# Two moves in the attention loop: ScalarE's high parts ahead of its copy of the transposed outputs, VectorE's shifted row ahead of the sums of squares

## The chip, the cores and the metric

The kernel runs on one core of one Trainium2 chip. The metric is the device time of one execution in microseconds (us), from 3 executions of the kernel before: 829.25, 830.49 and 831.02, so a median of 830.49.

## The reference, cut to what matters

The input `x` is 128 sequences of 64 tokens with 256 channels, and `cond` has one row of 256 per sequence. The reference is `x` plus one transformer block in which each linear layer stands between a log map and an exp map of hyperbolic space:

```
xn = layer_norm(logmap0(x))
xm = expmap0(xn * (1 + sc_msa) + sh_msa)
q, k, v = (_to_heads(plin(xm, w, b)) for w, b in ((w_q, b_q), (w_k, b_k), (w_v, b_v)))
scores = einsum('bhqd,bhkd->bhqk', logmap0(q), logmap0(k)) / sqrt(HD)
out_h = expmap0(einsum('bhqk,bhkd->bhqd', softmax(scores), logmap0(v)))
attn_out = plin(_from_heads(out_h), w_o, b_o)
x = mobius_add(residual, expmap0(g_msa * logmap0(attn_out)))
...
```

There are 16 heads of 16 channels. After the first half comes a second one of the same kind with two feed-forward layers. Every `logmap0` and `expmap0` needs the norm of a row, or of each head's 16 channels in a row; this is why the kernel sums squares by head and takes inverse roots.

## The kernel before, in words

Two sequences make a tile of 128 rows, so there are 64 tiles, and all of `x` stays in SBUF. The program has a set-up (weights, the modulation rows of `cond`, statistics of `x`), a first half (attention, tile by tile), a short stage of arithmetic for all rows at once, and a second half (feed-forward, two tiles at a time). The change touches the first half alone.

The first half is a software pipeline written out by hand. A slot is one step of it, and in each slot every stage works on another tile: with lag 0 (`L_A`) the layer norm's `modulate` and `shift_t`, with lag 1 (`L_B`) the transposes of `t`, with lag 2 (`L_C`) the projection to q, k and v, with lag 3 (`L_D`) `project`, `square_u`, `sum_squares`, `sum_rows`, `inverse_norms` and `head_roots`, with lag 4 (`L_E`) `limit`, `factors`, `scale_qk`, `high_parts`, `low_parts` and `repeat_parts`, with lag 5 (`L_H`) the transposes of q and k, the scores, the exponential and `attend`, with lag 6 (`L_L`) `softmax_sums`, `normalise`, `evac_oT` and the output projection, with lag 7 (`L_G`) the gate and the statistics. Each engine runs its own list of these calls in a fixed order, and an instruction waits on semaphores for what other engines (or its own earlier instructions) have made. So the order of the calls in `slot` (ScalarE, GpSimd, TensorE) and in `slot_until_rows` and `slot_from_bias` (VectorE) sets the order of the work.

Slots 0 to 7 and the last ones are written out; those between are a loop of two slots per pass. VectorE's loop is rotated: it is turned between the two parts of an even slot, so that the jump back (the instructions of L311) stands right behind `sum_rows` of each even slot and ahead of `gate_z`; an odd slot has no jump inside.

What the two moves and their neighbours do:

- `high_parts` (L614, ScalarE) rounds the scaled q and k (`qk`) to 16-bit floats in `qk4`. `low_parts` (L477, GpSimd) subtracts these from `qk` and stores the rests. `repeat_parts` (L1236 and L1237, VectorE) copies both to their second places, and only then can TensorE transpose them (L855), with which a slot begins on TensorE.
- `evac_oT` (L624, ScalarE) copies the transposed attention outputs out of PSUM, for the output projection (L872).
- `sum_squares` (L1167, VectorE) sums the squares that ScalarE made (`square_u`, L635) over each head's 16 channels, and `sum_rows` (L1171) sums those over the heads. ScalarE takes an estimate of the inverse roots of them (L646, L649), and GpSimd's five steps (L452, L454, L456, L458, L461) refine it to `roots`, which VectorE's `limit` (L1210) needs in the next slot.
- `modulate` (L1094, VectorE) writes `lnx`, and `shift_t` (L1145) makes `t` of it. It waits for `modulate` through the semaphore `ln_half`.
- `gate_z` (L1196, VectorE) multiplies the attention's result with the gate rows, with both inputs in SBUF; `dot_x` (L1203), `add_bo` (L1189) and `repeat_parts` follow.

```
dve.wait_ge(ln_half, i + 1)
...
dve.wait_ge(heads_summed, i + 1)
dve.tensor_reduce(hs[:, 3 * H:NF], hs[:, 0:3 * H].rearrange("p (a h) -> p a h", h=H), AX.X, ALU.add).then_inc(rows_summed, 1)
```

Of the kernel before, what the change touches and what calls it, by code (L numbers as in the profile page):

```python
# [52 lines left out]
def build(nc, x, cond, w_q, b_q, w_k, b_k, w_v, b_v, w_o, b_o, w_f1, b_f1, w_f2, b_f2, w_ada, b_ada, out):  # L53
# [16 lines left out]
    with ExitStack() as ctx:  # L70
# [216 lines left out]
        L_A, L_B, L_C, L_D, L_E, L_H, L_L, L_G = 0, 1, 2, 3, 4, 5, 6, 7  # L287
# [44 lines left out]
        def on(h, off, lag, items=T):  # L332

            return not isinstance(h, int) or 0 <= 2 * h + off - lag < items
# [222 lines left out]
        def _(act):  # L557
# [74 lines left out]
            def square_u(i, k):  # L632
                act.wait_ge(u_ready, i + 1)
                after(act, heads_summed, i)
                act.activation(usq[:, :], u[:, k, :], ACT.Square).then_inc(u_squared, 1)  # L635
# [33 lines left out]
            def slot(h, off):  # L669
                if on(h, off, L_H):  # L670
                    evac_qkT(2 * h + off - L_H)
                if on(h, off, L_B):
                    evac_tT(2 * h + off - L_B, (off - L_B) % 2)
                if on(h, off, L_D):
                    square_u(2 * h + off - L_D, (off - L_D) % 2)
                if on(h, off, L_L):
                    evac_oT(2 * h + off - L_L)
                if on(h, off, L_E):
                    high_parts(2 * h + off - L_E)
                if on(h, off, L_H):  # L680
                    exp_scores(2 * h + off - L_H)
                if on(h, off, L_D):
                    inverse_norms(2 * h + off - L_D)
                if on(h, off, L_A):
                    square_t(2 * h + off - L_A, (off - L_A) % 2)
                if on(h, off, L_G):
                    square_zg(2 * h + off - L_G, (off - L_G) % 2)
                if on(h, off, L_L):
                    square_z(2 * h + off - L_L, (off - L_L) % 2)

            run_tiles(act, slot)

            def scale_x(i, j):
# [303 lines left out]
        def _(dve):  # L997
# [241 lines left out]
            def slot_until_rows(h, off):  # L1239
# [11 lines left out]
                    scale_qk(2 * h + off - L_E, (off - L_E) % 2)  # L1251
                if on(h, off, L_A) and not at_start(h, off):
                    modulate(2 * h + off - L_A, (off - L_A) % 2, h + (off - L_A) // 2)
                if on(h, off, L_D):
                    sum_squares(2 * h + off - L_D)
                if on(h, off, L_A):
                    shift_t(2 * h + off - L_A, (off - L_A) % 2)
                if on(h, off, L_D):
                    sum_rows(2 * h + off - L_D)

            def slot_from_bias(h, off):
# [272 lines left out]
```

## Time and profile before

| what | value |
|---|---|
| median of 3 executions | 830.49 us |
| the profiled execution's own time | 829.5 us |
| its span in the profile | 827.7 us |
| granted TensorE clock, mean | 0.956 of full speed |
| busy share VectorE, TensorE (matmul), ScalarE, GpSimd | 86%, 84%, 70%, 43% |
| first half in its loop | about 95 to 500 us |

The profile is of one execution. Its page gives the busy time of each engine and the costliest groups of instructions; the trace behind it also answers for a stretch of time: each instruction's start and duration, who waited for whom, and the chain of work that ended last. PE is TensorE's matmul, PEld its load of weights, DVE VectorE, ACT ScalarE, POOL GpSimd; "DVEq" is VectorE's sequencer, which runs jumps and register instructions. An instruction of an engine can start shortly before the one ahead of it has ended, since they are pipelined.

### The profile page before, as it was taken

What the parts mean: (1) busy time and instruction counts of PE and PEld (TensorE: products, weight loads), DVE (VectorE), ACT (ScalarE), POOL (GpSimd) and SP (SyncE); (2) the same over time, 40 slices, a digit from 0 to 9 for tenths busy, and PEclk for the clock granted to TensorE, in tenths of its full rate; (3) what the DMA queues carried; (4) which work ended last, traced back from release to release, by engine and by line L of the source; (5) the groups of instructions that cost most, each with busy time, mean ns of one, the idle gap of its engine ahead of it and who ended that gap; (6) DMA issues with size and microseconds to landing.
All of it is one profiled execution on the core that took longest, in us unless ns stands there. A gap on an engine that the chain in (4) does not pass through costs nothing.

```text
span 827.7 us, 29731 instructions
## 1 busy us (share of the span) xinstructions
PE 691.9 (84%) x9393; PEld 514.0 (62%) x9393; DVE 715.3 (86%) x2231; ACT 580.6 (70%) x1627; POOL 355.9 (43%) x682
## 2 busy tenths in 40 slices
PE   5957999898999989999899999623778999889996
PEld 2746777777777777777777777511335555555555
DVE  3767899999999999999999999866988888888885
ACT  1125787777877777777778777633668888878874
POOL 1005555565555655555655556310233233233231
PEclk9969999999999999999999999955989999999999
DMA  9931111111112111111111110022343555455533
GB/s 325 358 83 61 39 54 58 57 55 46 51 57 57 57 45 52 55 57 57 49 50 53 57 57 21 24 68 65 86 116 109 136 153 145 127 136 154 143 100 102
DMA packets 51811, 73.99 MB, mean 89 GB/s; under 512 B 7081, under 2 KB 34609, under 8 KB 51762
## 3 DMA queue, kind: packets, MB, share of 16 engines
q1 hardware_dynamic: 49970, 70.55, 29.1%
q10 hardware_dynamic: 1792, 2.89, 1.0%
q8 instruction: 18, 0.29, 0.2%
q14 instruction: 31, 0.25, 0.1%
HBM read 64.24 MB, written 9.18 MB: 89 GB/s over the span
## 4 chain that ended last, share of the span: by engine, by line
issue 30%; PE 19%; DVE 19%; ACT 12%; DVEq 4%; DMA 3%; POOL 2%; SPq 1%; ACTq 0%; POOLq 0%
PE p_s L855 8%; ACT usq L635 5%; PE p_s L963 3%; ACT tT L630 3%; DVEq L50 2%; DMA mod_b<-mod_rows 2%; DVE qk L1237 2%; PE p_qkv L963 2%; DVE g_all L1196 1%; PE p_t L949 1%; DVE t L1145 1%; PE p_o L977 1%; PE p_o L976 1%; PE p_o L975 1%; DVE junk L1203 1%
## 5 line engine op out<-in xcount | busy, mean ns | idle before, releaser
L898 PE MATMUL p_qkv<-wqkv,tT 128*128 128x256 f32 x768 | 189.9, 385 | 2.0 <-DVE u L1161 2.0
L898 PEld LDWEIGHTS p_qkv<-wqkv,tT 128*128 128x128 f32 x768 | 136.4, 193 | 19.1 <-ACT tT L630 2.4
L477 POOL TENSOR_TENSOR qk<-qk 128x512 f16<-128x512 f32 x64 | 74.1, 1158 | 100.4 <-ACT qk L614 100.4
L619 ACT ACTIVATE qkT<-p_s 128x1024 f32<-128x1024 f32 x64 | 65.5, 1024 | 73.7 <-PE p_s L855 73.7
L855 PE MATMUL p_s<-ident,qk 128*128 128x128 f16 x1024 | 69.1, 221 | 32.7 <-DVE qk L1237 32.7
L912 PEld LDWEIGHTS p_o<-v,pT 64*64 64x64 f32 x4096 | 68.2, 136 | 36.0 <-issue 36.0
L912 PE MATMUL p_o<-v,pT 64*64 64x17 f32 x4096 | 72.6, 209 | 12.2 <-ACT pT L666 12.2
L855 PEld LDWEIGHTS p_s<-ident,qk 128*128 128x128 f16 x1024 | 58.0, 98 | 38.8 <-DVE qk L1237 38.7
L666 ACT ACTIVATE pT<-p_s 128x1024 f32<-128x1024 f32 x64 | 65.5, 1024 | 19.8 <-PE p_s L888 19.7
L1196 DVE SCALAR_TENSOR_TENSOR g_all<-z,gate 128x256 f32 (+1 forms) x64 | 63.9, 998 | 13.1 <-issue 13.1
L872 PE MATMUL p_oz<-wo,oT 128*128 128x256 f32 x256 | 74.2, 413 | 0.9 <-ACT oT L624 0.9
L1227 DVE TENSOR_TENSOR qk<-u,fac 128x256 f32<-128x256 f32 x128 | 70.5, 589 | 0.1
L445 POOL TENSOR_TENSOR rt<-ss_t,c_mhalf 128x1 f32<-128x1 f32 x64 | 46.8, 730 | 53.8 <-ACT junk L641 53.8
L504 POOL TENSOR_TENSOR rt<-ss,c_mhalf 128x2 f32<-128x2 f32 x32 | 24.3, 761 | 101.2 <-ACT wqkv L716 99.4
L1161 DVE SCALAR_TENSOR_TENSOR u<-p_qkv,ct,bqkv 128x768 f32<-128x768 f32 x64 | 64.3, 1005 | 2.9 <-PE p_qkv L898 2.9
L1167 DVE TENSOR_REDUCE hs<-usq 128x48 f32<-128x768 f32 x64 | 61.0, 952 | 4.0 <-ACT usq L635 1.6
L963 PE MATMUL p_qkv<-wff,qk 128*128 128x384 f32 (+1 forms) x128 | 58.8, 608 | 3.7 <-ACT qk L728 3.6
L949 PE MATMUL p_t<-ident,pT 128*128 128x128 f32 x128 | 20.7, 286 | 47.7 <-ACT pT L723 47.7
L510 POOL TENSOR_TENSOR rh<-hh,c_mhalf 128x2 f32<-128x2 f32 x32 | 26.3, 820 | 74.2 <-DVE hh L1381 74.2
L468 POOL TENSOR_TENSOR v<-u,fac 128x256 f32<-128x256 f32 x64 | 40.3, 629 | 36.2 <-DVE fac L1216 36.2
L963 PE MATMUL p_s<-wff,qk 128*128 128x384 f32 (+1 forms) x128 | 52.4, 552 | 4.1 <-ACT qk L728 4.1
L635 ACT ACTIVATE usq<-u 128x768 f32<-128x768 f32 x64 | 54.1, 846 | 0.8 <-DVE u L1161 0.8
(268 smaller groups left out, 1720.4 us busy)
## 6 DMA issues: line engine op xcount, KB each, us to landing
mod<-mod_rows SPq DMA_DIRECT2D x128, 128.0 KB, 2.9
x_all<-in_x SPq DMA_DIRECT2D x8, 1024.0 KB, 14.2
gate<-mod_rows SPq DMA_DIRECT2D x128, 64.0 KB, 2.5
mod<-mod_rows SPq DMA_DIRECT2D x32, 256.0 KB, 4.1
mod_b<-mod_rows SPq DMA_DIRECT2D x32, 256.0 KB, 4.1
out<-x_all SPq DMA_DIRECT2D x32, 256.0 KB, 2.2
gate<-gate_rows SPq DMA_DIRECT2D x32, 128.0 KB, 3.4
bqkv<-gate_rows SPq DMA_DIRECT2D x32, 128.0 KB, 3.9
```

The source lines that it names most:

```text
L477: pool.tensor_tensor(low, qk[:, :].rearrange("p (a h d) -> p a h d", a=2, d=HD), qk4[:, :, :, 0, :], ALU.subtract).then_inc(low_ready, 1)
L619: act.activation(qkT[:, :, :, :].rearrange("p a g n -> p (a g n)").bitcast(F32), p_s[:, :], ACT.Copy).then_inc(qkT_ready, 1)
L635: act.activation(usq[:, :], u[:, k, :], ACT.Square).then_inc(u_squared, 1)
L666: act.activation(pT[:, :, :, :].rearrange("p e g n -> p (e g n)"), p_s[:, :], ACT.Exp, scale=SCALE / (QK_UP * QK_UP)).then_inc(p_ready, 1)
L855: mm = pe.transpose(p_qkT[:, a, g, :], qk4[:, a, 2 * g:2 * g + 2, :, :].rearrange("p h r d -> p (h r d)"), ident16[:, :])
L872: mm = pe.matmul(p_oz[:, 0:D], oT[:, c, :, :].rearrange("p b s -> p (b s)"), wo[:, c, :], start=c == 0, stop=c == C - 1)
L898: mm = pe.matmul(p_qkv[:, a * D:a * D + D], tT[:, k, c, :], wqkv[:, c, a * D:a * D + D], start=c == 0, stop=c == C - 1)
L912: mm = pe.matmul(p_o[S * e:S * e + S, col:col + VW], pT[keys, e, g, :], v[keys, k, 2 * g + e, :], start=True, stop=True, skip_group_check= ...
L963: mm = pe.matmul((p_qkv, p_s)[k][:, 512 * j + c * P:512 * j + 512], t2T[:, k, j, c, :], wff[:, c, c * P:2 * D], start=False, stop=c == C - 1)
L1161: dve.scalar_tensor_tensor(out=u[:, k, :], in0=p_qkv[:, 0:3 * D], scalar=ct[:, k:k + 1], in1=bqkv[:, :], op0=ALU.mult, op1=ALU.add).then_i ...
L1196: dve.scalar_tensor_tensor(out=tile_of(g_all, i), in0=z[:, :], scalar=1.0, in1=gate[:, k, :], op0=ALU.mult, op1=ALU.mult, accum_out=st[:, ...
L1227: dve.tensor_tensor(qk[:, part].rearrange("p (h d) -> p h d", d=HD), u[:, k, part].rearrange("p (h d) -> p h d", d=HD), fac[:, a * H:a * H ...
```

## The change

ScalarE now makes the high parts before it copies the transposed outputs. VectorE now makes `t` right behind `lnx`, and the sums of squares behind `t`. No instruction is added or taken away, none changes its size, and no wait is changed.

```diff
@@ ScalarE, slot
                 if on(h, off, L_D):
                     square_u(2 * h + off - L_D, (off - L_D) % 2)
+                if on(h, off, L_E):
+                    high_parts(2 * h + off - L_E)
                 if on(h, off, L_L):
                     evac_oT(2 * h + off - L_L)
-                if on(h, off, L_E):
-                    high_parts(2 * h + off - L_E)
                 if on(h, off, L_H):
                     exp_scores(2 * h + off - L_H)
@@ VectorE, slot_until_rows
                 if on(h, off, L_A) and not at_start(h, off):
                     modulate(2 * h + off - L_A, (off - L_A) % 2, h + (off - L_A) // 2)
-                if on(h, off, L_D):
-                    sum_squares(2 * h + off - L_D)
                 if on(h, off, L_A):
                     shift_t(2 * h + off - L_A, (off - L_A) % 2)
                 if on(h, off, L_D):
+                    sum_squares(2 * h + off - L_D)
                     sum_rows(2 * h + off - L_D)
```

VectorE's list before, in an odd slot of the loop, from `modulate` to `gate_z` (ISA and REGISTER_ALU are instructions of the sequencer):

```order
L1094 SCALAR_TENSOR_TENSOR lnx<-x_all,arrays,mod 128x256
L1167 TENSOR_REDUCE hs<-usq 128x48 [waits roots_ready,u_squared]
L1142 REGISTER_ALU
L1145 ISA [waits t_squared,tT_psum,ln_half]
L1145 SCALAR_TENSOR_TENSOR t<-lnx,arrays,mod 128x256
L1171 TENSOR_REDUCE hs<-hs 128x3 [waits heads_summed]
L1194 ISA [waits z_ready]
L1196 ISA [waits stats_kept,gate_in0]
L1196 SCALAR_TENSOR_TENSOR g_all,st<-z,gate 128x256
```

The same place in the changed kernel:

```order
L1094 SCALAR_TENSOR_TENSOR lnx<-x_all,arrays,mod 128x256
L1142 REGISTER_ALU
L1145 ISA [waits t_squared,tT_psum,ln_half]
L1145 SCALAR_TENSOR_TENSOR t<-lnx,arrays,mod 128x256
L1167 TENSOR_REDUCE hs<-usq 128x48 [waits roots_ready,u_squared]
L1171 TENSOR_REDUCE hs<-hs 128x3 [waits heads_summed]
L1194 ISA [waits z_ready]
L1196 ISA [waits stats_kept,gate_in0]
L1196 SCALAR_TENSOR_TENSOR g_all,st<-z,gate 128x256
```

The large sum (L1167) has moved behind `t` with nothing between it and the small sum that waits for it (L1171), and the sequencer's instruction that waits for `ln_half` now follows `lnx` directly.

ScalarE's list before, in the first slot of a pass of its loop:

```order
L635 ACTIVATE usq<-u 128x768 [waits heads_summed]
L50 REGISTER_ALU [waits oT_psum]
L624 ACTIVATE oT<-p_oz 128x2x2x64 [waits z_psum]
L610 ISA
L614 ACTIVATE qk<-qk 128x32x16 [waits low_ready,again_ready,qkT_psum,qk_ready]
L666 ACTIVATE pT<-p_s 128x1024 [waits o_psum,s_psum]
```

And in the changed kernel:

```order
L635 ACTIVATE usq<-u 128x768 [waits heads_summed]
L610 ISA
L614 ACTIVATE qk<-qk 128x32x16 [waits low_ready,again_ready,qkT_psum,qk_ready]
L50 REGISTER_ALU [waits oT_psum]
L624 ACTIVATE oT<-p_oz 128x2x2x64 [waits z_psum]
L666 ACTIVATE pT<-p_s 128x1024 [waits o_psum,s_psum]
```

The copy of the outputs, with the register instruction that waits for TensorE's transposes, has moved behind the high parts.

## Rows read from the trace of the kernel before

**Rows 1.** The page, busy time of each engine over the span.

```profile
PE 691.9 (84%) x9393; PEld 514.0 (62%) x9393; DVE 715.3 (86%) x2231; ACT 580.6 (70%) x1627; POOL 355.9 (43%) x682
```

**Rows 2.** Waits of 100 to 500 us: who for whom, total us, times, longest.

```profile
POOL qk L477 <- ACT qk L614: 88.3, 55, 1.7
```

**Rows 3.** Timeline of an odd slot: start us, us, engine, line, operation.

```profile
308.57 1.07 PE L855 MATMUL p_s<-ident,qk 128*128 128x128 f16 x16 [0.56 <-DVE qk L1237]
309.40 0.17 DVE L1210 TENSOR_TENSOR rlim<-roots,c_lim 128x3 f32<-128x3 f32 x1
310.86 0.85 ACT L635 ACTIVATE usq<-u 128x768 f32<-128x768 f32 x1
311.21 0.47 DVE L1094 SCALAR_TENSOR_TENSOR lnx<-x_all,arrays,mod 128x256 f32<-128x256 f32 x1
311.74 0.95 DVE L1167 TENSOR_REDUCE hs<-usq 128x48 f32<-128x768 f32 x1
311.85 0.38 ACT L624 ACTIVATE oT<-p_oz 128x256 f32<-128x256 f32 x1
312.13 0.62 ACT L614 ACTIVATE qk<-qk 128x512 f16<-128x512 f32 x1
...
312.98 1.16 POOL L477 TENSOR_TENSOR qk<-qk 128x512 f16<-128x512 f32 x1 [1.61 <-ACT qk L614]
313.12 1.30 DVE L1196 SCALAR_TENSOR_TENSOR g_all<-z,gate 128x256 f32 x1
314.35 0.08 DVE L1196 DVE_READ_ACCUMULATOR g_all<-z,gate 128x1 f32 x1
314.72 0.40 POOL L452 TENSOR_TENSOR nw<-y 128x51 f32<-128x51 f32 x1 [0.58 <-ACT y L649]
...
315.89 1.07 PE L855 MATMUL p_s<-ident,qk 128*128 128x128 f16 x16 [0.48 <-DVE qk L1237]
316.40 0.29 POOL L461 TENSOR_TENSOR roots<-nw,c_fac 128x51 f32<-128x51 f32 x1
316.72 0.17 DVE L1210 TENSOR_TENSOR rlim<-roots,c_lim 128x3 f32<-128x3 f32 x1
```

**Rows 4.** Timeline of the even slot before it, the same columns.

```profile
301.18 1.07 PE L855 MATMUL p_s<-ident,qk 128*128 128x128 f16 x16 [0.48 <-DVE qk L1237]
...
302.01 0.16 DVE L1210 TENSOR_TENSOR rlim<-roots,c_lim 128x3 f32<-128x3 f32 x1
303.92 0.47 DVE L1094 SCALAR_TENSOR_TENSOR lnx<-x_all,arrays,mod 128x256 f32<-128x256 f32 x1
304.42 0.95 DVE L1167 TENSOR_REDUCE hs<-usq 128x48 f32<-128x768 f32 x1
305.29 0.47 DVE L1145 SCALAR_TENSOR_TENSOR t<-lnx,arrays,mod 128x256 f32<-128x256 f32 x1
305.69 0.19 DVE L1171 TENSOR_REDUCE hs<-hs 128x3 f32<-128x48 f32 x1
306.36 0.74 DVE L1196 SCALAR_TENSOR_TENSOR g_all<-z,gate 128x256 f32 x1 [0.48 <-issue]
```

**Rows 5.** Line 311 from 304 to 308 us: operation, duration ns, start.

```profile
L311 DVEq ALU_OP  x1: 40/40/40, 305.4 to 305.4; - x1
```

**Rows 6.** Chain of waits, the sequencer's instruction ahead of the gate, even slot, then odd.

```profile
306.23 0.08 DVEq L1196
312.92 0.06 DVEq L1196
```

**Rows 7.** Lines 1196 and 456 over the span: duration ns min/median/max, first and last start.

```profile
L1196 DVE SCALAR_TENSOR_TENSOR g_all<-z,gate x64: 412/970/1423, 92.5 to 545.4; 128x256 f32 x54, 128x256 f32<-128x256 f32 x10
L456 POOL TENSOR_TENSOR nw<-nw,c_three x64: 275/407/412, 67.5 to 526.7; 128x51 f32<-128x51 f32 x64
```

## The prediction

> **What bounds the kernel now.** The page comes first [rows 1]: VectorE is busy for 86% of the span and TensorE for 84%, so neither can be called idle, and the shares don't say which wait ends last. The waits of the loop come next [rows 2]: GpSimd waits for the high parts 55 times, 88.3 us in all. That is a long wait of an engine that has time, and it says only that the low parts start as soon as they can. The timelines show what hangs on that start [rows 3, 4]. I read each as distances from T, the start of TensorE's transposes of q and k.
>
> In the odd slot T is 308.57 and the next T is 315.89, 7.32 us later. ScalarE's squares start at T+2.29, its copy of the outputs at T+3.28, the high parts at T+3.56. The low parts start 0.23 after these have ended, at T+4.41, and end at T+5.57. VectorE begins its gate product (L1196) at T+4.55, and it takes 1.30 us, where the shortest of its kind takes 0.41 [rows 7]. Its accumulator is read at T+5.78, 0.21 after the low parts have ended. So this product stands still while GpSimd runs, and from the read to the next T there are another 1.54 us of VectorE's work (the products and copies that end in L1237). The even slot has the same pattern and 7.39 us. **So the chain squares, copy, high parts, low parts, gate product sets the length of both slots**, and a pair of slots takes 14.71 us.
>
> A second chain is tied with it. GpSimd's five steps towards the roots start at T+6.15 and end at 316.69, and VectorE's `limit` follows at 316.72, which is T+8.15 and also 0.83 behind the next T [rows 3]. It has hardly any slack. Nothing that the change moves stands between T and those five steps (TensorE's order, the exponential), so this chain doesn't get shorter with the first.
>
> **ScalarE's move.** The high parts now start behind the squares. Neighbours on ScalarE overlap by 0.10 us (the copy, 0.38 long, starts 0.28 ahead of the high parts), so the high parts start at 2.29 + 0.85 - 0.10 = T+3.04, 0.52 earlier: 0.28 for the copy and 0.24 that the copy had waited for TensorE and for its issue. The low parts then run from 3.04 + 0.62 + 0.23 = T+3.89 to T+5.05. The copy of the outputs ends by T+3.94 instead of T+3.66. The projection that needs it starts at about T+4.4, behind the scores, and this covers the 0.28; without that cover it would be paid once in each slot.
>
> **VectorE's move, the odd slot.** `t` now follows `lnx` directly and needs its result. The sequencer's instruction that waits for it can run only when `lnx` has ended: I take 0.47 for `lnx`, 0.05 until the sequencer goes on (the large sum of the even slot ends at 305.37, and the sequencer's next instruction is at 305.4 [rows 4, 5]), 0.06 for its instruction and 0.05 until the engine starts (306.23 + 0.08 against 306.36 [rows 4, 6]). So `t` starts 0.63 behind `lnx`. The large sum follows 0.40 later (as L1171 behind L1145 [rows 4]) and takes 0.95. Before, the sum stood 0.53 behind `lnx`, so it now ends about 0.50 later. In the odd slot, with `lnx` at T+2.64, the sum ends at T+4.62. The gate product can start 0.34 after that (312.69 to 312.92 + 0.06 + 0.05 [rows 3, 6]), at T+4.96. The low parts end at T+5.05, so they still decide: accumulator at T+5.26, next T at 5.26 + 1.54 = **6.80, where it was 7.32**. `t` itself is read out before T+3.89, so it doesn't meet the low parts; the large sum does. The small sum ran 0.19 long beside the low parts [rows 4], so I don't charge the large one. The Trainium skill (SBUF — State Buffer, section "Who interferes with whom") says that a reduction never contends with GpSimd and that an instruction with two SBUF inputs does; the trace agrees for the small sum and the gate product, and if the large sum stood still as that product does, the odd slot would get no shorter at all.
>
> **The even slot.** Here the jump back of the loop lies between the small sum and the gate product. The jump's first instruction is at 305.4, right behind the end of the large sum (305.37), though `t` had been handed over long before: the sequencer stood at the small sum, which waits for the large one. From the end of the large sum to the gate product there are 0.99 us [rows 4]. Before, `t` ran inside this stretch and the low parts covered the rest. Now `t` is ahead of it and the stretch is bare. Counted from `limit`: `lnx` at +1.91, `t` 0.63, sum 0.40, its length 0.95, jump 0.99, so the gate product starts at +4.88 (before: 306.36 - 302.01 = +4.35). The low parts end near +4.1, so it runs unhindered: 0.34 to the accumulator, then 1.54, and the next T is at +6.76. Before it was 308.57 - 302.01 = +6.56. **The even slot becomes longer by 0.20, counted from `limit`.**
>
> **The sum.** With odd slots of 6.80 the even slot's `limit` no longer waits for VectorE (6.80 + 0.83 = T+7.63) but for the roots. Before they allowed T+8.15. Two of the five steps were slowed by VectorE's copies: the shortest L456 takes 0.28 and the median 0.41 [rows 7], and L452 took 0.40 [rows 3]. If nothing met any more, 0.25 would go: T+7.90. The copies now come 0.52 earlier beside the same steps and meet L452 and L454, so I expect one of the two delays to stay, T+8.00. A pair then takes 8.00 + 6.76 = 14.76 us against 14.71. The loop has 27 passes (slots 8 to 61), so + 0.05 x 27 = +1.4 us. The bounds are T+7.90 (pair 14.66, -1.4 us) and T+8.15 with one more 0.10 where a GpSimd step delays a copy (pair 15.01, +8 us).
>
> The slots that are written out have no jump. There the earlier low parts help, some 2 to 3 slots of them by 0.4: -1.0 us, with 0 and -2.1 (four slots by 0.52) as bounds. Against the profiled execution this gives 829.5 + 1.4 - 1.0 = 829.9; the median of the runs stands 1.0 higher, so 830.9, and I say 830.8.
>
> **Rivals.**
> - **A, the jump stays hidden: much faster.** If the sequencer hands over the small sum and runs the jump while that still waits, the even gate product waits for the low parts alone: the high parts at about +2.04 from `limit`, low parts to +4.05, accumulator +4.26, next T at +5.80. Two slots could then take 13.80. The chain through the roots, one `limit` to the next (309.40 to 316.72, 7.32), gives back perhaps 0.2 in a slot, so I take 14.2: -0.5 x 27 = -14 us, 816 us. Against it stands the jump at 305.4 [rows 5], which had no reason to wait until then except the sum. The Trainium skill (Perfetto Trace Analysis, section "DVE / Act Engine Instruction (TENSOR_ADD, Activation, etc)") says that an instruction is pushed into a wait queue and the sequencer is then ready to decode the next one; by that rule this rival would come true. The row speaks for a held sequencer.
> - **B, the roots are made earlier: a little faster.** If none of GpSimd's steps meets a copy and the written-out slots give their full gain, -1.4 and -2.1: about 827 us. It needs the copies to fall between the steps.
> - **C, slower.** The bound of the pair's sum: two of GpSimd's steps stay slowed in the odd slot, and a copy (L1236 or L1237) is held back by a step, since each takes what the other needs. `limit` of the even slot at T+8.15 and 0.10 more: +8 us, less the ends, 837 us. It decides from T+8.07 on, where a pair is 0.12 longer than before and 27 pairs cost 3.2 us.
> - **D, the change does nothing.** The high parts would start no earlier if something else held them, such as `qk` (ready at about T+2.73). It is ready before T+3.04, so I give this no chance of its own.
>
> **How the numbers follow.** 0.2% is 1.7 us, about what a measurement of this kernel can tell from no change. The forecast (pair 14.70 to 14.83) has 0.46, A 0.14, B 0.15, C 0.25. The forecast's own range is 829 to 833 and is mostly "same" (0.34), with 0.05 faster and 0.07 slower. Together: faster 0.34, same 0.34, slower 0.32. The range leaves out A and the far end of C: 825 to 836.5.
>
> **What would show it.** In an odd slot the low parts should start near T+3.9 and the next T come near 6.8. In an even slot `lnx`, `t` and the large sum should stand 0.63 and 0.40 apart, the gate product should be 0.4 long with an idle time before it that ends by "issue", and the slot should take nearly 8 us, with `limit` now waiting for the roots. GpSimd's wait for the high parts should shrink by about 0.5 an entry. I am wrong if even slots are below 7.4, if the large sum is longer than 0.95, or if a pair is under 14.5 or over 15.1.

## The result, and the profile after

The changed kernel takes 830.99 us (median of 20 runs, 826.81 to 834.55) against 828.45 us of the kernel before in the same sessions (20 runs, 826.37 to 831.3). The ratio is 1.0029, with a 95% interval of 1.0019 to 1.0039: slower by 0.3%, by more than noise and by less than half a per cent. The time lies 0.2 us from the predicted one. Since the kernel before ran 2.0 us faster than the median I started from, the step I had forecast (+0.4 us) was in fact +2.5.

The page of the profiled execution of the changed kernel (831.02 us, span 829.2, mean granted clock 0.952) answers to [rows 1].

```profile
PE 699.0 (84%) x9379; PEld 515.6 (62%) x9393; DVE 686.1 (83%) x2231; ACT 576.6 (70%) x1627; POOL 348.4 (42%) x682
```

VectorE is busy for 29 us less, and the kernel is no faster. A product that stands still counts as busy, so most of this is standing still that has turned into idle time. The lines of the gate product and of L456 say it more plainly (duration in ns as min/median/max, first and last start); they answer to [rows 7].

```profile
L1196 DVE SCALAR_TENSOR_TENSOR g_all<-z,gate x64: 410/427/1160, 90.0 to 546.8; 128x256 f32 x54, 128x256 f32<-128x256 f32 x10
...
L456 POOL TENSOR_TENSOR nw<-nw,c_three x64: 275/277/407, 66.1 to 525.7; 128x51 f32<-128x51 f32 x64
```

The median gate product took 970 ns before and takes 427 now, and the median L456 went from 407 to 277. The contention that the change aims at is gone. The waits of 100 to 500 us (who for whom, total us, times, longest) show where its time went; the first row answers to [rows 2].

```profile
POOL qk L477 <- ACT qk L614: 54.1, 54, 1.1
...
DVE g_all L1196 <- issue: 19.6, 26, 0.8
DVE rlim L1210 <- POOL roots L461: 11.2, 28, 0.4
```

GpSimd waits 0.6 us an entry less for the high parts. VectorE waits 0.75 us in each pass ahead of the even gate product (26 times) and 0.40 for the roots ahead of the even limit (28 times). The timeline of the changed kernel over an even slot, an odd slot and the start of the next pair answers to [rows 4] and [rows 3].

```profile
299.22 1.05 PE L855 MATMUL p_s<-ident,qk 128*128 128x128 f16 x16 [0.17 <-issue]
300.26 0.16 DVE L1210 TENSOR_TENSOR rlim<-roots,c_lim 128x3 f32<-128x3 f32 x1 [0.40 <-POOL roots L461]
...
302.17 0.47 DVE L1094 SCALAR_TENSOR_TENSOR lnx<-x_all,arrays,mod 128x256 f32<-128x256 f32 x1
...
302.79 0.48 DVE L1145 SCALAR_TENSOR_TENSOR t<-lnx,arrays,mod 128x256 f32<-128x256 f32 x1
...
303.18 1.15 POOL L477 TENSOR_TENSOR qk<-qk 128x512 f16<-128x512 f32 x1 [0.86 <-ACT qk L614]
303.19 0.95 DVE L1167 TENSOR_REDUCE hs<-usq 128x48 f32<-128x768 f32 x1
...
305.12 0.43 DVE L1196 SCALAR_TENSOR_TENSOR g_all<-z,gate 128x256 f32 x1 [0.75 <-issue]
...
307.03 1.07 PE L855 MATMUL p_s<-ident,qk 128*128 128x128 f16 x16 [0.78 <-DVE qk L1237]
307.82 0.15 DVE L1210 TENSOR_TENSOR rlim<-roots,c_lim 128x3 f32<-128x3 f32 x1
...
310.91 1.15 POOL L477 TENSOR_TENSOR qk<-qk 128x512 f16<-128x512 f32 x1 [1.14 <-ACT qk L614]
...
311.91 0.43 DVE L1196 SCALAR_TENSOR_TENSOR g_all<-z,gate 128x256 f32 x1
...
312.74 1.12 PE L912 MATMUL p_o<-v,pT 64*64 64x17 f32 x64 [0.17 <-ACT pT L666]
...
314.03 1.05 PE L855 MATMUL p_s<-ident,qk 128*128 128x128 f16 x16 [0.17 <-issue]
315.06 0.16 DVE L1210 TENSOR_TENSOR rlim<-roots,c_lim 128x3 f32<-128x3 f32 x1 [0.40 <-POOL roots L461]
```

The even slot now takes 307.03 - 299.22 = 7.81 us and the odd slot 7.00: a pair of 14.81 against 14.71. In the loop no gate product stands still any more (0.44 us at most), and the even one is bare behind its 0.75 of idle time. What VectorE's sequencer does in this idle time stands in the chain of waits of the changed kernel (start us, us, instruction):

```profile
304.17 0.05 DVE hs L1171
...
304.25 0.06 DVEq L311
304.31 0.26 issue
304.57 0.06 DVEq L311
...
304.69 0.06 DVEq L1194
...
304.99 0.08 DVEq L1196
...
305.12 0.10 DVE g_all L1196
```

As in [rows 4, 5], the jump (L311) begins when the large sum has ended (303.19 + 0.95 = 304.14) and not before, and the gate product starts 0.98 us behind that end. In the odd slot, which has no jump, the same distance is 0.33 us (the sum runs from 310.63 to 311.58, the gate product starts at 311.91), so the jump itself adds 0.65.

What the whole execution makes of this can be read from three transposes: the one of slot 8 (the loop's first), of slot 62 (the first behind it) and the last one. Before:

```profile
95.15 0.23 PE L855 MATMUL p_s<-ident,qk 128*128 128x128 f16 x1 [0.26 <-DVE qk L1237]
...
492.47 0.23 PE L855 MATMUL p_s<-ident,qk 128*128 128x128 f16 x1 [0.48 <-DVE qk L1237]
...
532.44 0.23 PE L855 MATMUL p_s<-ident,qk 128*128 128x128 f16 x1
```

And after:

```profile
92.10 0.23 PE L855 MATMUL p_s<-ident,qk 128*128 128x128 f16 x1
...
491.68 0.22 PE L855 MATMUL p_s<-ident,qk 128*128 128x128 f16 x1 [0.17 <-issue]
...
534.16 0.29 PE L855 MATMUL p_s<-ident,qk 128*128 128x128 f16 x1
```

The loop took 397.32 and takes 399.58 us: +2.26, that is 0.084 in each of 27 pairs. Slot 8 comes 3.05 us earlier, and the written-out end takes 2.51 us longer (39.97 and 42.48). Both ends are mixed with the granted clock of TensorE. In the end it fell earlier in this execution of the changed kernel; the seventh number of the windows of before is the clock (first came busy us and instructions of PE, PEld, DVE, ACT and POOL):

```profile
524.00:530.00 6.00, 4.16 (x119) 3.18 (x119) 5.36 (x18) 4.34 (x11) 3.50 (x8) 1.00 0.08 25
530.00:536.00 6.00, 3.21 (x88) 2.58 (x84) 4.90 (x15) 3.12 (x7) 1.39 (x2) 1.00 0.08 26
```

And of after, the same windows:

```profile
524.00:530.00 6.00, 5.32 (x117) 4.36 (x115) 4.43 (x17) 3.23 (x10) 2.71 (x8) 0.52 0.09 25
530.00:536.00 6.00, 5.85 (x99) 4.63 (x88) 3.33 (x9) 2.15 (x6) 1.34 (x2) 0.50 0.10 26
```

At the lower of its two levels (1.2 GHz) TensorE is busy for 11.2 of the 12 us, where it was busy for 7.4 at 2.4 GHz. So the 2.51 us at the end can't be read as a cost of the order. At the start it was the kernel before that had a stretch at the lower level (granted clock 0.66 from 79 to 84 us, 1.00 after the change).

### The profile page after: what moved, and what is told of

Read it like the earlier page. It is cut to its first block, busy times and chain, and to the rows that moved or that the text cites. A ratio compares the mean times of both kernels' runs of the same rounds, so it can differ in the third digit from the quotient of the medians.

```text
span 829.2 us, 29717 instructions
## 1 busy us (share of the span) xinstructions
PE 699.0 (84%) x9379; PEld 515.6 (62%) x9393; DVE 686.1 (83%) x2231; ACT 576.6 (70%) x1627; POOL 348.4 (42%) x682
## 4 chain that ended last, share of the span: by engine, by line
DVE 32%; issue 27%; PE 15%; POOL 7%; DMA 5%; ACT 4%; DVEq 4%; SPq 4%; POOLq 1%; ACTq 0%
DVE hs L1167 6%; DVE qk L1227 4%; DVE lnx L1094 3%; SPq L365 3%; PE p_s L963 3%; PE p_qkv L898 3%; DVEq L50 2%; DVE u L1161 2%; DMA x_all<-in_x 2%; DMA mod<-mod_rows 2%; DMA mod_b<-mod_rows 2%; POOL nw L452 1%; DVE rden L1176 1%; PE p_t L949 1%; PE p_qkv L963 1%
## 5 line engine op out<-in xcount | busy, mean ns | idle before, releaser
L898 PE MATMUL p_qkv<-wqkv,tT 128*128 128x256 f32 x768 | 194.3, 386 | 2.3 <-DVE u L1161 2.0
L898 PEld LDWEIGHTS p_qkv<-wqkv,tT 128*128 128x128 f32 x768 | 134.5, 191 | 25.8 <-issue 9.2
L477 POOL TENSOR_TENSOR qk<-qk 128x512 f16<-128x512 f32 x64 | 74.0, 1157 | 62.8 <-ACT qk L614 62.8
L912 PEld LDWEIGHTS p_o<-v,pT 64*64 64x64 f32 x4096 | 69.6, 139 | 35.7 <-issue 35.7
L912 PE MATMUL p_o<-v,pT 64*64 64x17 f32 x4096 | 74.2, 211 | 11.5 <-ACT pT L666 11.5
L872 PE MATMUL p_oz<-wo,oT 128*128 128x256 f32 x256 | 75.4, 418 | 1.7 <-ACT oT L624 1.5
L504 POOL TENSOR_TENSOR rt<-ss,c_mhalf 128x2 f32<-128x2 f32 x32 | 23.7, 741 | 101.6 <-ACT wqkv L716 101.6
L963 PE MATMUL p_qkv<-wff,qk 128*128 128x384 f32 (+1 forms) x128 | 58.5, 605 | 3.6 <-ACT qk L728 3.6
L1167 DVE TENSOR_REDUCE hs<-usq 128x48 f32<-128x768 f32 x64 | 60.6, 947 | 0.3 <-ACT usq L635 0.3
L963 PE MATMUL p_s<-wff,qk 128*128 128x384 f32 (+1 forms) x128 | 52.4, 552 | 4.1 <-ACT qk L728 4.1
L452 POOL TENSOR_TENSOR nw<-y 128x51 f32<-128x51 f32 x64 | 21.7, 339 | 80.6 <-ACT y L649 80.6
```

Source lines behind the costliest of these rows:

```text
L477: pool.tensor_tensor(low, qk[:, :].rearrange("p (a h d) -> p a h d", a=2, d=HD), qk4[:, :, :, 0, :], ALU.subtract).then_inc(low_ready, 1)
L872: mm = pe.matmul(p_oz[:, 0:D], oT[:, c, :, :].rearrange("p b s -> p (b s)"), wo[:, c, :], start=c == 0, stop=c == C - 1)
L898: mm = pe.matmul(p_qkv[:, a * D:a * D + D], tT[:, k, c, :], wqkv[:, c, a * D:a * D + D], start=c == 0, stop=c == C - 1)
L912: mm = pe.matmul(p_o[S * e:S * e + S, col:col + VW], pT[keys, e, g, :], v[keys, k, 2 * g + e, :], start=True, stop=True, skip_group_check= ...
L963: mm = pe.matmul((p_qkv, p_s)[k][:, 512 * j + c * P:512 * j + 512], t2T[:, k, j, c, :], wff[:, c, c * P:2 * D], start=False, stop=c == C - 1)
L1167: dve.tensor_reduce(hs[:, 0:3 * H], usq[:, :].rearrange("p (a d) -> p a d", d=HD), AX.X, ALU.add).then_inc(heads_summed, 1)
```

## The experiments

After the result, one claim of the prediction carried the whole explanation: the jump of the loop is exposed in the even slot because the sequencer stands at the small sum. What each half of the change does alone, the prediction didn't say. Here are the twelve runs; every edit is to VectorE's or ScalarE's order or to the place of the jump. The pair is read from the transposes of the loop in each trace. The time of the kernel before differs between sessions (825.82 to 828.45), so the ratio is the one to compare. The loop makes 27 pairs, and their sum is a second measure: the second half, which no edit touches, takes 248.3 to 255.8 us in these profiled executions (from its first product, L963, to the end).

| kernel | us (before) | ratio, 95% interval | pair, us |
|---|---|---|---|
| before | | 1 | 14.71 |
| the change | 830.99 (828.45) | 1.0029 [1.0019, 1.0039] | 14.80 |
| ScalarE's half alone | 824.93 (828.20) | 0.9964 [0.9952, 0.9977] | 14.55 |
| VectorE's half alone | 831.64 (828.20) | 1.0052 [1.0038, 1.0066] | 14.93 |
| change + small sum behind the gate product | 814.20 (828.20) | 0.9837 [0.9823, 0.9852] | 14.17 |
| change + jump further ahead | 817.83 (828.20) | 0.9865 [0.9846, 0.9883] | 14.27 |
| new order of VectorE in odd slots only, small sum ahead | 815.22 (825.82) | 0.9876 [0.9845, 0.9908] | 14.28 |
| before + small sum behind the gate product | 812.37 (825.82) | 0.9833 [0.9799, 0.9867] | 14.20 |
| change + small sum behind + outputs ahead of the limit ("the fastest") | 803.01 (825.82) | 0.9731 [0.9698, 0.9764] | 13.92 |
| change + outputs ahead of the limit | 846.69 (827.83) | 1.0215 [1.0167, 1.0263] | 15.27, some longer |
| the fastest, ScalarE's half undone | 823.98 (827.83) | 0.9952 [0.9936, 0.9968] | 14.66 |
| the fastest, VectorE's half undone | 824.46 (827.83) | 0.9959 [0.9944, 0.9974] | 14.59 |
| the fastest, both halves undone | 839.37 (827.70) | 1.0135 [1.0117, 1.0153] | 15.14 |
| the fastest, limit between the outputs' two steps | 805.34 (827.70) | 0.9724 [0.9705, 0.9743] | 13.82 |

### The halves alone

ScalarE's half alone, against the kernel before (the copy of the outputs lies between the two places):

```diff
+                if on(h, off, L_E):
+                    high_parts(2 * h + off - L_E)
...
-                if on(h, off, L_E):
-                    high_parts(2 * h + off - L_E)
```

> ScalarE's move alone; VectorE keeps the order of the kernel before. My theory (the sequencer is held by the small sum, so the jump of the even slot is bare once nothing stands in it): here shift_t still stands between the two sums, so the even slot's gate product starts 4.35 behind limit, unhindered, the accumulator is read at 4.69 and the next slot begins 6.23 behind limit. With limit at T+8.00 a pair takes about 14.2 us, 0.5 less than before: about -13 us, 815 to 818. Rival (the chain through the roots holds everything): no gain, a pair of 14.7 us and a time within 0.2% of the kernel before.

It gave 3 us and not 13. The timeline shows why:

```profile
300.82 0.95 DVE L1167 TENSOR_REDUCE hs<-usq 128x48 f32<-128x768 f32 x1
...
301.55 1.15 POOL L477 TENSOR_TENSOR qk<-qk 128x512 f16<-128x512 f32 x1 [1.07 <-ACT qk L614]
...
301.69 1.29 DVE L1145 SCALAR_TENSOR_TENSOR t<-lnx,arrays,mod 128x256 f32<-128x256 f32 x1
```

The low parts come earlier, as meant, and now catch `t`, which was issued 0.14 after them and takes 1.29 where it takes 0.47 [rows 4]. The one that stands still has changed, not that one does. This is what VectorE's half is for: it brings `t` ahead of the low parts. I had taken the two halves for independent.

VectorE's half alone:

```diff
+                if on(h, off, L_A):
+                    shift_t(2 * h + off - L_A, (off - L_A) % 2)
                 if on(h, off, L_D):
                     sum_squares(2 * h + off - L_D)
-                if on(h, off, L_A):
-                    shift_t(2 * h + off - L_A, (off - L_A) % 2)
                 if on(h, off, L_D):
                     sum_rows(2 * h + off - L_D)
```

> VectorE's move alone. My theory: the odd slot stays at 7.32 (the low parts end at T+5.57, after the gate product could start at T+4.96), the even slot takes 6.76 from limit instead of 6.56, so a pair takes 14.9 us, 0.2 more than before: +5 us. Rival (the order of shift_t and the sum is free, since the low parts cover both): the time of the kernel before, within 0.2%.

It came out nearly as forecast: the odd slot keeps its 7.32, and the even slot pays the bare jump and has 7.61.

### Is it the held sequencer?

Two edits take the jump away from behind the waiting small sum. The first puts the small sum behind the gate product, so that nothing that waits for the large sum stands ahead of the jump:

```diff
                 if on(h, off, L_D):
                     sum_squares(2 * h + off - L_D)
-                    sum_rows(2 * h + off - L_D)
 
             def slot_from_bias(h, off):
                 if on(h, off, L_G):
                     gate_z(2 * h + off - L_G, (off - L_G) % 2, h + (off - L_G) // 2)
+                if on(h, off, L_D):
+                    sum_rows(2 * h + off - L_D)
```

> The changed kernel, with sum_rows moved behind gate_z. Now no waiting instruction stands between the large sum and the jump. My theory (the sequencer is held at the instruction that waits, not at the one that runs): the jump goes on beside the large sum, the even gate product starts when the low parts end, about 4.05 behind limit instead of 4.86, and the even slot loses about 0.7 us. Then TensorE and the roots bound, some 7.0 to 7.1 a slot, a pair of 14.1: about -17 us against the changed kernel, 812 to 816. Rival (the idle time of 0.75 before the gate product is the fetch behind the jump, whatever stands before it): the product stays near 4.8 behind limit and the time at 831.

Measured: 16 to 17 us less than the changed kernel (0.019 by the ratios, 0.63 us in each of 27 pairs), as the theory said. The chain of waits of this run, in an even slot:

```profile
308.20 0.04 DVEq L311
...
308.48 0.18 DVE hs L1167
...
308.71 0.06 DVEq L1194
...
308.91 0.08 DVEq L1196
...
309.34 0.17 DVE g_all L1196
```

The jump begins at 308.20, 0.28 us before the large sum starts, and the sequencer is at the gate's line (L1194) at 308.71, while that sum still runs (to 309.43). After the change it was there only 0.55 us behind the sum's end. The gate product starts 3.79 behind the limit (309.34 against 305.55), where it stood at +4.86. It meets the low parts again (308.60 to 309.76) and takes 0.70, and the slot is 6.83 long instead of 7.81.

The second edit leaves all instructions in their order and moves only the jump, to between the products with the factors and the modulation:

```diff
                     scale_qk(2 * h + off - L_E, (off - L_E) % 2)
+
+            def slot_from_bias(h, off):
                 if on(h, off, L_A) and not at_start(h, off):
                     modulate(2 * h + off - L_A, (off - L_A) % 2, h + (off - L_A) // 2)
...
                     sum_rows(2 * h + off - L_D)
-
-            def slot_from_bias(h, off):
                 if on(h, off, L_G):
                     gate_z(2 * h + off - L_G, (off - L_G) % 2, h + (off - L_G) // 2)
```

> The changed kernel, with the turn of VectorE's loop moved: the jump now stands between scale_qk and modulate, where two products of 1.1 us in all are still running; the order of the computing instructions is the same as in the changed kernel. My theory: the jump hides, the even slot becomes like the odd one (6.8 to 7.1), a pair takes about 14.1 us, about -17 us against the changed kernel. Rival (the even slot is long for another reason, such as the order of the two sums or TensorE): a pair stays at 14.8 and the time at 831.

It gave 13 to 14 of the 17 us. Since the engine's order is the same word for word, this part can only be the place of the jump. It keeps 0.23 of idle time ahead of one gate product in each pair (6.0 us in 26), which may be why it has 14.27 and not 14.17; no run separates that.

### Two controls

VectorE's new order in odd slots only, where no jump lies, with ScalarE's move in all slots and the small sum where the change has it, ahead of the gate product:

```diff
+                if on(h, off, L_D) and off == 0:
+                    sum_squares(2 * h + off - L_D)
                 if on(h, off, L_A):
                     shift_t(2 * h + off - L_A, (off - L_A) % 2)
-                if on(h, off, L_D):
+                if on(h, off, L_D) and off == 1:
                     sum_squares(2 * h + off - L_D)
```

> ScalarE's move in all slots; VectorE's new order in odd slots alone, the old one (the large sum, shift_t, the small sum, the jump) in even slots. My theory: the jump's stretch is filled again by shift_t, which now stands still until the low parts have ended (two SBUF inputs, 1.29 in e1_high_only), so the even slot takes 6.48 from limit as there instead of 6.76; with limit at T+8.0 a pair takes 14.5, -0.3 against the changed kernel: -8 us, 821 to 824. Rival (the loss of the even slot isn't in the order of shift_t and the sum): 831.

The gain over the changed kernel was about one and a half times what I expected (the pair 0.51 shorter instead of 0.3, the ratio 0.9876), though in the even slots `t` stands still behind the low parts (1.18 and 1.19 us in two of them). Without the bare jump an even slot of 7.29 with one stall is still shorter than 7.81.

And the kernel before with the small sum behind the gate product and nothing of the change:

```diff
...
-                if on(h, off, L_D):
-                    sum_rows(2 * h + off - L_D)
 
             def slot_from_bias(h, off):
                 if on(h, off, L_G):
                     gate_z(2 * h + off - L_G, (off - L_G) % 2, h + (off - L_G) // 2)
+                if on(h, off, L_D):
+                    sum_rows(2 * h + off - L_D)
```

> The kernel before with sum_rows moved behind gate_z, and neither move of the change: the control for e3. My theory: here the low parts cover the jump, so freeing the sequencer gains nothing; the small sum now follows the gate product, on the path, and costs its 0.11 in each of some 54 slots, +4 to +6 us: 832 to 834. Rival (moving the small sum is a gain of its own, whatever the order of the rest): about -14 us, as e3.

Here my theory missed: I had expected +4 to +6 and it was 14 us faster, about as fast as the first edit on top of the change. The timeline of an odd slot shows a mechanism that I had not seen:

```profile
303.03 1.46 POOL L477 TENSOR_TENSOR qk<-qk 128x512 f16<-128x512 f32 x1 [1.54 <-ACT qk L614]
303.05 0.42 DVE L1196 SCALAR_TENSOR_TENSOR g_all<-z,gate 128x256 f32 x1
...
303.61 1.16 DVE L1203 SCALAR_TENSOR_TENSOR junk<-x_all,g_all 128x256 bf16 x1
```

The gate product and the low parts start 0.02 us apart by the records. The product runs at its full speed, and it is GpSimd that stands still, for 0.30 (1.46 instead of 1.16). Then GpSimd has its turn, and the product with x (L1203), 0.42 long elsewhere, takes 1.16. The even slot does the same (L477 1.40, L1203 1.17). In the kernel before, the small sum had held the gate product back: in the odd slot from T+4.43 to T+4.55, just enough for the low parts to be first [rows 3], and in the even slot, where the jump stood behind the small sum, from T+4.52 to T+5.18. So the small sum had cost the kernel before time in two ways, and what its move gains there (14 us) isn't the jump's alone. With the small sum behind the gate product the change itself is worth nothing that the times show: 0.9837 with it, 0.9833 without, pairs of 14.17 and 14.20. With the change VectorE then waits for the roots 57 times (23.7 us), and without it once. The run with only the jump moved is the one that separates the jump.

### A faster version, and what the change is worth there

VectorE's reciprocal and its scaling of the outputs (`softmax_sums` and `normalise`, in the places left out below) now stand ahead of the limit and the factors, on top of the change with the small sum behind:

```diff
-                if on(h, off, L_E):
-                    limit(2 * h + off - L_E)
...
-                if on(h, off, L_E):
-                    factors(2 * h + off - L_E)
...
+                if on(h, off, L_E):
+                    limit(2 * h + off - L_E)
+                if on(h, off, L_E):
+                    factors(2 * h + off - L_E)
```

> The kernel of e3_small_sum_behind_gate, with softmax_sums and normalise ahead of limit and factors. My theory of what bounds e3: from limit (which waits for the roots) over the normalised outputs to TensorE, the exponential and back to the roots, about 7.1 a slot. Here the outputs no longer wait for limit, so TensorE's own order bounds, 6.8 to 6.9 a slot: a pair of 13.7 to 13.8 against 14.17, -10 to -12 us against e3, 802 to 805. Rival (e3 is bound by TensorE already): no change within 0.3%, 814.

803.01 us, a ratio of 0.9731 to the kernel before. The time is the expected one, but the bound isn't: I had expected TensorE's own order and a pair of 13.7 to 13.8. VectorE's waits of 100 to 500 us are nearly gone:

```profile
DVE fac L1216 <- DVE rlim L1210: 10.6, 54, 0.2
DVE t L1145 <- DVE lnx L1094: 4.3, 27, 0.2
```

It waits neither for the roots nor for the issue of the gate product, so its own chain is now the bound: 6.93 and 6.99 us a slot. I then took the edit alone, on the changed kernel, with the small sum where the change has it (the diff is the one just shown, and nothing else):

> The changed kernel with one more edit: VectorE's reciprocal and its scaling of the outputs stand ahead of the limit, the products with it and the modulation; the small sum stays in front of the gate product. Theory (the even slot is set by the limit, that is by GpSimd's roots, and by the stretch from there to the next T; 0.65 us of that stretch is the reciprocal and outputs, which can be done while VectorE waits for the roots): the stretch from limit to next T shrinks by about 0.6, but the limit itself stands at T+1.0 only if the roots allow, so the pair of slots loses about 0.2 to 0.3 us against 14.80: 14.55 to 14.6, and the time is 4 to 8 us under the changed kernel, about 824 to 827. Rival 1 (the whole gain of the outputs move comes here too): 11 us less, about 820. Rival 2 (the loop's jump behind the held sequencer bounds the pair alone): no change, 831.

All three expectations were wrong: it takes 16 us more than the change. The timeline of an odd slot shows a VectorE that doesn't wait for another engine, with gaps of its own:

```profile
303.16 0.15 DVE L1210 TENSOR_TENSOR rlim<-roots,c_lim 128x3 f32<-128x3 f32 x1
...
303.50 0.21 DVE L1216 TENSOR_TENSOR fac<-roots,rlim 128x48 f32<-128x48 f32 x1 [0.20 <-DVE rlim L1210]
...
303.75 1.19 DVE L1227 TENSOR_TENSOR qk<-u,fac 128x256 f32<-128x256 f32 x2
```

From the reciprocal (302.54) to `lnx` (304.86) there are 2.32 us; from the limit to `lnx`, with reciprocal and outputs in between, the odd slot of the changed kernel needs 309.61 - 307.82 = 1.79. The limit, the factors and the products each need the one before; the reciprocal and the outputs had stood between them and filled the gaps. Of these 0.53 us the trace shows 0.20 as idle and 0.12 in the products (1.19 instead of 1.07); the rest is starts that overlap less. In the even slot the way from limit to `lnx` was 1.91, so 0.41 is lost there. The changed kernel had only the 0.40 of waiting in every second slot to set against it: pairs of 15.27. TensorE now waits over 1.1 us for L1237 ahead of its transposes in 19 of the 27 passes, and behind seven of these waits its granted clock fell; VectorE then waited up to 0.9 us for TensorE (L1189 for L872). Why it fell behind these seven and not behind the others no run shows. The windows of one such pass:

```profile
114.00:118.00 4.00, 3.42 (x23) 3.06 (x24) 3.73 (x11) 2.47 (x6) 2.40 (x6) 0.64 0.27 98
118.00:122.00 4.00, 3.83 (x51) 2.76 (x50) 2.82 (x10) 2.18 (x5) 1.34 (x2) 0.93 0.01 3
```

Such a slot takes up to 8.69 us instead of 7.31, and the mean pair of the loop is 15.51. The same edit pays in the fastest version. Two things differ there, and no run tells their shares apart. The kernel that it was made on waited for the roots in both slots (23.7 us in 57 entries, against 11.2 in 28 after the change), so there was more idle time to give; and it has no bare jump.

The last four runs ask what the change itself is worth where VectorE is the bound. Its halves were undone one at a time and then together (first ScalarE's, then VectorE's, then the two diffs together):

```diff
-                if on(h, off, L_E):
-                    high_parts(2 * h + off - L_E)
...
+                if on(h, off, L_E):
+                    high_parts(2 * h + off - L_E)
```
```diff
-                if on(h, off, L_A):
-                    shift_t(2 * h + off - L_A, (off - L_A) % 2)
...
+                if on(h, off, L_A):
+                    shift_t(2 * h + off - L_A, (off - L_A) % 2)
```

> The fastest version so far (803 us, pair 13.93) with ScalarE's two instructions back in the old order: the copy of the outputs ahead of the high parts. Theory (the high parts 0.5 earlier free GpSimd earlier, so that the gate product and what follows it start earlier, also once no small sum holds the sequencer): the low parts come 0.5 later, gate product or dot stands still behind them, pair about 14.2, time 7 to 10 us longer, about 811. Rival (in this version the products run under GpSimd's cover anyway): the same 803 within 2 us.

> The fastest version so far (803 us, pair 13.93) with VectorE's two instructions back in the old order: the sums of squares ahead of the shifted row. Theory (the shifted row reads two operands from SBUF and is issued just after the low parts start, so it stands still until they end, as in the run with ScalarE's move alone): its record lengthens from 0.48 to about 1.2 to 1.3 us, pair about 14.3, time 8 to 12 us longer, about 812. Rival (without the small sum ahead of it the gate product takes the loss up): the same 803 within 2 us.

> The fastest version so far (803 us, pair 13.93) with both halves of the change undone: copy of the outputs ahead of the high parts, sums of squares ahead of the shifted row. Each half undone alone gave 824 (pairs 14.66 and 14.59), because one instruction of VectorE stood still behind the low parts: the gate product 0.94 us, or the shifted row 1.16. Theory (VectorE has no idle time in this version, so a stall there is added to the slot in full; the two halves gain only together): the shifted row is just done before the low parts, and the gate product stands still, pair 14.6 to 14.7, 822 to 826 us. Rival (the halves act each by itself and add up): 845, pair 15.3.

Each half undone costs 18 to 20 us, twice what I expected, and both cost 33. (The ratios are 0.022, 0.023 and 0.040 above that of the fastest, and the loops are 19.8, 17.9 and 32.9 us longer; the plain times, 21, 21 and 36 us apart, come from different sessions.) The gate product and `t` over the whole span, in the fastest version:

```profile
L1196 DVE SCALAR_TENSOR_TENSOR g_all<-z,gate x64: 409/532/1329, 89.1 to 521.0; 128x256 f32 x54, 128x256 f32<-128x256 f32 x10
...
L1145 DVE SCALAR_TENSOR_TENSOR t<-lnx,arrays,mod x64: 483/484/487, 54.8 to 477.5; 128x256 f32<-128x256 f32 x64
```

With ScalarE's half undone the median gate product takes 846 ns instead of 532:

```profile
L1196 DVE SCALAR_TENSOR_TENSOR g_all<-z,gate x64: 412/846/1402, 91.9 to 544.7; 128x256 f32 x54, 128x256 f32<-128x256 f32 x10
```

With VectorE's half undone it is `t` that takes 1151 instead of 484:

```profile
L1145 DVE SCALAR_TENSOR_TENSOR t<-lnx,arrays,mod x64: 475/1151/1229, 54.3 to 497.5; 128x256 f32<-128x256 f32 x64
```

With both undone it is the gate product again:

```profile
L1196 DVE SCALAR_TENSOR_TENSOR g_all<-z,gate x64: 413/1374/1403, 92.3 to 558.7; 128x256 f32 x54, 128x256 f32<-128x256 f32 x10
```

GpSimd loses time there too: the low parts start just behind `t` and take 1.36 and 1.44 us instead of 1.16. My theory for that run was that the halves gain only together (822 to 826 us), and the rival that they add up (845). Neither is right, but the rival is much nearer: the second half to be undone costs 13 to 15 us, after 18 to 20 for the first. The change that costs 2.5 us in the given kernel is therefore worth about 33 where no jump lies bare and VectorE is the bound.

The last run sets the limit between the reciprocal and the scaling of the outputs, to fill the gap ahead of the factors:

```diff
-                if on(h, off, L_L):
-                    normalise(2 * h + off - L_L)
                 if on(h, off, L_E):
                     limit(2 * h + off - L_E)
+                if on(h, off, L_L):
+                    normalise(2 * h + off - L_L)
...
```

> The fastest version so far (803 us, pair 13.93) with the limit set between the reciprocal and the scaling of the outputs, so that the factors no longer follow the limit as its dependent neighbour (0.20 us idle ahead of the factors in that version, in each slot). Theory (VectorE's own chain is the bound, so idle time between dependent neighbours counts in full): 0.20 goes per slot, but GpSimd's roots end only 0.15 to 0.2 after the reciprocal is done, which takes back half or more; pair 13.7 to 13.85, 797 to 801 us. Rival (the roots bound the slot, so that the limit waits for as long as was saved): 803 within 1.5 us.

The gap ahead of the factors is gone in the timeline, and one of 0.24 has opened ahead of the limit, which now waits for the roots. The loop is 2.5 us shorter (373.4 against 375.9), but the times don't show it: the second half, which the edit doesn't touch, takes 255.8 us in this profiled execution and 250.0 in that of the fastest. The ratios 0.9724 and 0.9731 lie within each other's intervals, so whether this edit gains anything in the whole stays open.

## Why the prediction was right, and where it wasn't

**The time and the sign.** 830.8 was predicted and 830.99 measured. That the two lie 0.2 us apart is luck: the median I started from was 2.0 us too high, and the step of +0.4 us that I added was 2.1 too small. The measured step of +2.5 lies beyond the 0.2% that I had called no change. It is at the upper end of the forecast case (829 to 833, up to 2.5 above the 830.49 I started from), and its pair of 14.80 is inside that case's 14.70 to 14.83.

**The even slot: right.** The gate product was to start 4.88 behind the limit and to run unhindered, with the next T at +6.76. Measured: +4.86, 0.43 long, +6.77. `t` came 0.62 behind `lnx` (0.63), the sum 0.40 later (0.40) and 0.95 long (0.95). The wait ended by "issue" is there, 0.75 long, in 26 of the passes.

**The limit at T+8.00: right within its bounds.** It came at T+8.03 (315.06 - 307.03), so the pair became 14.80 instead of the forecast 14.76, and 0.084 instead of 0.05 times 27 made +2.3 instead of +1.4 us. With the ends (-0.5 instead of -1.0) the two profiled executions are 1.7 us apart at the last transpose; where the rest of the 2.5 between the medians comes from, no trace shows. The working behind it, one of GpSimd's two delays staying, held as well: in the odd slot L452 still takes 0.41, and L456 is at 0.28.

**The odd slot: the mechanism right, a floor missed.** I had 6.80 and it took 7.00. The low parts came at T+3.88 (T+3.89) and the gate product was done early enough; L1237 ended at 313.74. But the next transposes started only at 314.03, 0.17 after TensorE's own L912 had ended, with the reason "issue". TensorE's order had become the last to end, and I hadn't looked at what is late next on that engine. It cost nothing here, because the next limit waits for the roots anyway. It matters once the jump is hidden: with only the jump moved the odd slot takes 6.99.

**The written-out slots: not shown.** The term of -1.0 us stands in the profiled pair as -3.05 ahead of the loop and +2.51 behind it, -0.5 together. Both are mixed with stretches at TensorE's lower clock that came at different places in the two executions, so the term is neither confirmed nor refuted.

**The rivals.** A, the hidden jump, fell: the jump still starts at the end of the large sum. The Trainium skill (Perfetto Trace Analysis, section "DVE / Act Engine Instruction (TENSOR_ADD, Activation, etc)") says that the sequencer is ready for the next instruction once it has pushed one into the wait queue. The traces here don't agree: the sequencer's next work starts at 305.4 and 304.2, when the awaited sum has ended. Two runs that took the wait from ahead of the jump gained 13 and 17 us. What rival A would have given is what they give: 817.83 and 814.20, where I had 816. B and C differ from the forecast only in the roots; the measured pair is 0.04 above my forecast, on the side of C.

**What was not in the prediction at all** is why the halves belong together, and that the kernel before paid for its small sum in both slots. I had read the gate product's stall as given by the time of the low parts. It is given by which of the two starts first, and in the odd slot this the small sum decided. The records can't order them more finely than some hundredths of a us: where they start 0.02 apart, GpSimd lost though its record is the earlier one.

## What to carry to other kernels

An instruction that waits for its own neighbour also holds everything the sequencer has to do behind it; put nothing of that kind right ahead of a loop's jump. When an edit frees an engine and the time doesn't move, look for what that engine now waits on in the slot with the jump, and try the edit again once that is gone: the same two moves cost 2.5 us in one surrounding, gained nothing that shows in a second and about 33 us in a third. Before gathering dependent steps side by side, count what stood between them, for on a bound engine it was free filling.

## What the runs showed of the hardware

- VectorE's sequencer stands at an instruction whose wait isn't met, and does no register work or jump meanwhile; from the end of the awaited sum to the gate product there are 0.98 to 0.99 us with the jump between them and 0.33 without, so a bare jump costs 0.65 here.
- Of two instructions that read two SBUF operands each, one on VectorE and one on GpSimd, one stands still until the other is done. Mostly it is the one that starts later (a gate product behind the low parts takes 1.30 instead of 0.43, `t` 1.29 instead of 0.47), and GpSimd can be the loser: 1.46 us instead of 1.16 with a gate product that starts 0.02 us from it by the records. A reduction ran 0.95 long beside the low parts (303.18 and 303.19) as without them. The Trainium skill (SBUF — State Buffer, section "Who interferes with whom") says that such a VectorE instruction contends with a GpSimd instruction that reads SBUF, that the order of issue decides who blocks, and that a reduction never contends. The trace agrees.
- VectorE's two 16-bit copies (L1236, L1237), which read one operand, meet GpSimd's small steps too: in the kernel before, L456 and L1237 both start at 315.56, and L456 takes 0.41 instead of 0.28.
- Two small steps of VectorE of which the second needs the first (limit and factors) leave 0.20 us idle between them, 54 times of 54 (10.6 us in the fastest version); with an independent step in between, as in the changed kernel, no such idle time is recorded.
